# One full-height product and one paired product in the fold of an attention block

## What is computed

```
W = weights[condition]                          # (B, 32, 32)
h = einsum('bct,bcd->bdt', x, W)
q_c = h @ Wq_c.T + bq_c                         # 192 query latents
q = q_c @ Wq_up.T + bq_up                       # 32 heads of 128 + 64
kv = h @ Wkv_c.T + bkv_c                        # 64 latents + 64 rotary
k = [kv_nope @ Wk_up.T, kv_rope];  v = kv_nope @ Wv_up.T
out = softmax(q @ k.T / sqrt(192)) @ v @ Wo.T + bo
```

## Time and profile before

| | |
|---|---|
| Median of 3 runs | 732.34 us (731.35 to 732.41) |
| The profiled execution | 729.96 us, span 728.1 us |
| Mean granted TensorE clock over the span | 0.998 |
| Busy, share of the span | PE 97%, PEld 78%, DVE 83%, ACT 57%, POOL 29% |
| The chain that ended last | PE 72%, DVE 15%, of it line L729 32% |
| Matmuls of the fold (L729) | 2304 |

### The profile page before, as it was taken

One profiled execution on the slowest core, in us unless ns is written; L12 is line 12 of the kernel. 1 busy time (PEld: TensorE's weight loads), 2 busy tenths in 40 slices (PEclk: granted clock), 3 DMA queues, 4 the chain that ended last, 5 costly groups with the idle time before them and its releaser, 6 DMA issues.

```text
span 728.1 us, 17041 instructions
## 1 busy us (share of the span) xinstructions
PE 705.8 (97%) x7154; PEld 567.8 (78%) x7154; DVE 601.3 (83%) x1010; ACT 412.7 (57%) x736; POOL 208.1 (29%) x237
## 2 busy tenths in 40 slices
PE   8999999999999999999999999999988899999997
PEld 6867777786978697777878786978666688888885
DVE  4889999998999777797769776787889689999975
ACT  4676565656556765746475565656645444444443
POOL 5461020020002010640110000004300257777784
PEclk9999999999999999999999999999999999999999
DMA  7800100010002001000100010002112487989943
GB/s 225 322 3 2 58 7 1 2 62 3 1 2 62 3 2 49 11 5 13 59 5 1 2 59 2 2 1 92 59 60 54 121 234 147 187 236 196 238 104 109
DMA packets 31919, 50.94 MB, mean 70 GB/s; under 512 B 6594, under 2 KB 21090, under 8 KB 30562
## 3 DMA queue, kind: packets, MB, share of 16 engines
q1 hardware_dynamic: 29858, 49.26, 25.0%
q0 software_dynamic: 1024, 0.53, 0.3%
q10 hardware_dynamic: 960, 0.06, 0.1%
HBM read 41.19 MB, written 8.63 MB: 68 GB/s over the span
## 4 chain that ended last, share of the span: by engine, by line
PE 72%; DVE 15%; issue 4%; ACT 4%; DMA 3%; POOL 2%; SPq 0%; DVEq 0%; ACTq 0%; POOLq 0%
PE ps L729 32%; PE ps L778 6%; PE ps L621 5%; PE ps L622 5%; PE ps L623 5%; PE ps L800 4%; PE ps L670 3%; PE ps L629 2%; PE ps L631 2%; PE ps L630 2%; DVE x_low L1654 2%; DVE x_t L1648 2%; PE ps L1022 1%; PE ps L1030 1%; DMA x_t<-in_x_channels 1%
## 5 line engine op out<-in xcount | busy, mean ns | idle before, releaser
L1134 ACT ACTIVATE qt<-ps,m_bias 128x512 f32<-128x512 f32 x228 | 145.9, 687 | 87.7 <-PE ps L729 86.9
L729 PE MATMUL ps<-q_high,m_high 64*128 64x512 f32 x768 | 165.0, 397 | 0.0
L729 PE MATMUL ps<-q_high,m_low 64*128 64x512 f32 x768 | 161.3, 387 | 0.0
L729 PE MATMUL ps<-q_low,m_high 64*128 64x512 f32 x768 | 113.8, 387 | 0.0
L729 PEld LDWEIGHTS ps<-q_high,m_high 64*128 64x128 f32 x768 | 88.7, 184 | 15.0 <-issue 5.5
L729 PEld LDWEIGHTS ps<-q_high,m_low 64*128 64x128 f32 x768 | 88.8, 184 | 9.2
L1422 DVE TENSOR_TENSOR z_low<-ps,z_high 128x512 fp32r<-128x512 f32 x128 | 79.8, 683 | 18.1 <-ACT z_high L1154 16.5
L729 PEld LDWEIGHTS ps<-q_low,m_high 64*128 64x128 f32 x768 | 81.1, 184 | 10.2
L1154 ACT CAST z_high<-ps 128x512 fp32r<-128x512 f32 x128 | 66.8, 597 | 14.6 <-PE ps L800 9.8
L1139 ACT ACTIVATE sc<-sc 128x512 f32<-128x512 f32 x60 | 38.1, 635 | 41.5 <-DVE sc L1407 41.4
L494 POOL TENSOR_TENSOR o_sum<-o_part,o_part 128x512 f32<-128x512 f32 x7 | 9.1, 1300 | 173.2 <-ACT o_part L1164 173.2
(11 more groups left out here) (259 smaller groups left out, 1468.7 us busy)
## 6 DMA issues: line engine op xcount, KB each, us to landing
x_raw<-in_x_groups SPq DMA_DIRECT2D x32, 256.0 KB, 4.0
x_t<-in_x_channels SPq DMA_DIRECT2D x8, 1024.0 KB, 7.9
out<-rest SPq DMA_DIRECT2D x32, 256.0 KB, 6.3
toep_high<-taps_scratch SPq DMA_DIRECT2D x32, 192.0 KB, 4.5
toep_low<-taps_scratch SPq DMA_DIRECT2D x32, 192.0 KB, 4.9
w_raw<-in_w_groups SPq DMA_DIRECT2D x8, 512.0 KB, 7.5
toep_far<-taps_scratch SPq DMA_DIRECT2D x32, 64.0 KB, 5.7
rope_raw<-in_rope_rows SPq DMA_DIRECT2D x8, 192.0 KB, 7.4
```

What stands on the lines that cost most here:

```text
L729: mm = pe.matmul(ps[:, fold_bank(u, j) + e, :], weights[rows, (GH * g + j) // 2, c, :], moving[c][rows, :], start=start, stop=stop)
L1134: act.activation(qt[:, j, :], ps[:, fold_bank(u, j) + j % 2, :], ACT.Identity, bias=m_bias[:, h:h + 1]).then_inc(s["qt_done"], 1)
```

## The change

The 192 latents of a head become one piece of 128 and one of 64. The piece of 128 is a full-height matmul for each head (`full`, L737 of the changed kernel); the last 64 of two heads are a pair on the two halves (`paired`, L743). A couple is 6 full-height matmuls and 3 pairs. `q_high` and `q_low` are one tile each for the first 128 latents; `qc_high` and `qc_low` hold the last 64 on both halves. They are mixed once for each token: the even features go to rows 0 to 63 and the odd ones to rows 64 to 127 of PSUM (L675), and ACT and DVE then cross 64 rows of 256 elements instead of 512. The second copy of 64 feature columns goes. The weight products become four of full height and four of half (L706, L709), and the host's layouts follow. The waits of the first fold on `q_done` and `q_crossed` move behind the full-height matmuls.

```diff
-    feat = t("feat", [P, 4, 64 + FEAT], at=qt_at + 24 * KB)
-    q_high, q_low = ([t(f"q_{part}{n}", [P, ST], F32R, at=(q_at + (2 * k + n) * 2 * KB if n < 2 else h_at + 2 * k * KB))
-                      for n in (0, 2, 1)] for k, part in enumerate(("high", "low")))
+    feat = t("feat", [P, 4, FEAT], at=qt_at + 24 * KB)
+    q_high, q_low, qc_high, qc_low = (t(name, [P, ST], F32R, at=q_at + 2 * n * KB) for n, name in
+                                      enumerate(("q_high", "q_low", "qc_high", "qc_low")))
...
+    halves = lambda tile: tile[:].rearrange("p (m d c) -> p d m c", d=2, c=P)
+    weight_of = lambda tile, h, slot: tile[:, 2 * (h // 4) + slot // 3, slot % 3, :]
...
-                for part, made in enumerate(("q_ready", "qca_ready", "kv_ready")):
-                    for n in range(4):
-                        mm = pe.matmul(mixed_in(part)[:, P * n:P * n + P], feat[:, n, P * part:P * part + P],
-                                       mix[n // 2][:, n % 2, :], start=True, stop=True)
-                    mm.then_inc(s[made], 1)
+                for n in range(4):
+                    mm = pe.matmul(mixed_in(0)[:, P * n:P * n + P], feat[:, n, 0:P], mix[n // 2][:, n % 2, :],
+                                   start=True, stop=True)
+                mm.then_inc(s["q_ready"], 1)
+                for n in range(4):
+                    mm = pe.matmul(mixed_in(1)[64 * (n % 2):64 * (n % 2) + 64, P * (n // 2):P * (n // 2) + P],
+                                   feat[:, n, P:QL], mix[n // 2][:, n % 2, :], start=True, stop=True)
+                mm.then_inc(s["qc_ready"], 1)
+                for n in range(4):
+                    mm = pe.matmul(mixed_in(2)[:, P * n:P * n + P], feat[:, n, QL:FEAT], mix[n // 2][:, n % 2, :],
+                                   start=True, stop=True)
+                mm.then_inc(s["kv_ready"], 1)
...
-                for p in range(2):
-                    for c in range(3):
-                        for e in range(2):
-                            j, part = 2 * p + e, (c + e) % 3
-                            pe.matmul(ps[64 * e:64 * e + 64, bank, 64 * (3 * p + c):64 * (3 * p + c) + 64],
-                                      w_raw[g][:, QL * j + 64 * part:QL * j + 64 * part + 64],
-                                      w_raw[g][:, 4 * QL + KVL * j:4 * QL + KVL * (j + 1)], start=True, stop=True)
+                key = lambda j: w_raw[g][:, 4 * QL + KVL * j:4 * QL + KVL * (j + 1)]
+                for j in range(4):
+                    pe.matmul(ps[:, bank, 64 * j:64 * j + 64], w_raw[g][:, QL * j:QL * j + P], key(j), start=True, stop=True)
+                for j in range(4):
+                    e, p = j % 2, j // 2
+                    pe.matmul(ps[64 * e:64 * e + 64, bank, 256 + 64 * p:256 + 64 * p + 64],
+                              w_raw[g][:, QL * j + P:QL * j + QL], key(j), start=True, stop=True)
...
-                def both(j, weights, moving, c, start=False, stop=False):
+                def full(j, weights, moving, start=False):
+                    for e in range(2):
+                        pe.matmul(ps[:, fold_bank(u, j) + e, :], weight_of(weights, GH * g + j, j % 4 + e), moving[:],
+                                  start=start, stop=False)
+
+                def paired(j, weights, moving, stop=False):
                     for e in range(2):
                         rows = slice(64 * e, 64 * e + 64)
-                        mm = pe.matmul(ps[:, fold_bank(u, j) + e, :], weights[rows, (GH * g + j) // 2, c, :],
-                                       moving[c][rows, :], start=start, stop=stop)
+                        mm = pe.matmul(ps[:, fold_bank(u, j) + e, :], weight_of(weights, GH * g + j, 4 + j % 4 // 2)[rows, :],
+                                       moving[rows, :], start=False, stop=stop)
                         if stop:
                             mm.then_inc(s["t_ready"], 1)
 
@@ -738,24 +752,21 @@
                         pe.wait_ge(s["s_taken"], 4)
                     if u < 2 and j % 4 == 0:
                         pe.wait_ge(s["fold_done"], (GH * g + j) // 4 + 1)
-                    for c in (0, 2, 1):
-                        if c == 2 and g == 0 and j == 0:
-                            pe.wait_ge(s["q_high_done"], 2 * k + 2)
-                        if c == 1 and g == 0 and j == 0:
-                            pe.wait_ge(s["q_crossed"], 2 * k + 2)
-                        both(j, m_high, q_high, c, start=(c == 0))
-                        both(j, m_low, q_high, c)
+                    full(j, m_high, q_high, start=True)
+                    full(j, m_low, q_high)
 
                 def by_low(j):
-                    if g == 0 and j == 0:
+                    first = g == 0 and j == 0
+                    if first:
                         pe.wait_ge(s["q_done"], 2 * k + 1)
-                    both(j, m_high, q_low, 0)
-                    if g == 0 and j == 0:
-                        pe.wait_ge(s["q_done"], 2 * k + 2)
-                    both(j, m_high, q_low, 2)
-                    if g == 0 and j == 0:
+                    full(j, m_high, q_low)
+                    if first:
+                        pe.wait_ge(s["q_crossed"], 2 * k + 2)
+                    paired(j, m_high, qc_high)
+                    paired(j, m_low, qc_high)
+                    if first:
                         pe.wait_ge(s["q_copied"], 2 * k + 2)
-                    both(j, m_high, q_low, 1, stop=True)
+                    paired(j, m_high, qc_low, stop=True)
...
-                act.copy(feat[:, n, 64:64 + FEAT], ps[:, FEAT_BANK[n], 0:FEAT])
-                act.copy(feat[:, n, 0:64], ps[:, FEAT_BANK[n], P:QL]).then_inc(s["feat_done"], 1)
+                act.copy(feat[:, n, :], ps[:, FEAT_BANK[n], 0:FEAT]).then_inc(s["feat_done"], 1)
...
-            def projected_ca(k):
-                act.wait_ge(s["qca_ready"], k + 1)
-                act.activation(q_high[2][:], mixed_in(1), ACT.Identity,
-                               bias=bq_c[:, 1:2]).then_inc(s["q_high_done"], 1)
+            def projected_c(k):
+                act.wait_ge(s["qc_ready"], k + 1)
+                for e in range(2):
+                    rows = slice(64 * e, 64 * e + 64)
+                    made = act.activation(halves(qc_high)[rows, e],
+                                          mixed_in(1)[rows, 0:HALF].rearrange("p (m c) -> p m c", c=P), ACT.Identity,
+                                          bias=bq_c[rows, 1:2])
+                made.then_inc(s["q_high_done"], 1)
 
             def crossed(k):
                 act.wait_ge(s["q_high_done"], 2 * k + 2)
-                act.copy(q_high[1][64:P, :], f(q_high[2][0:64, :])).then_inc(s["q_crossed"], 1)
-                act.copy(q_high[1][0:64, :], f(q_high[0][64:P, :])).then_inc(s["q_crossed"], 1)
+                for e in range(2):
+                    here, there = slice(64 * e, 64 * e + 64), slice(64 - 64 * e, P - 64 * e)
+                    act.copy(halves(qc_high)[there, e], f(halves(qc_high)[here, e])).then_inc(s["q_crossed"], 1)
...
                 dve.wait_ge(s["q_high_done"], 2 * k + 2)
-                dve.scalar_tensor_tensor(out=q_low[2][:], in0=mixed_in(1), scalar=bq_c[:, 1:2],
-                                         in1=f(q_high[2][:]), op0=ALU.add,
-                                         op1=ALU.subtract).then_inc(s["q_done"], 1)
+                for e in range(2):
+                    rows = slice(64 * e, 64 * e + 64)
+                    made = dve.scalar_tensor_tensor(out=halves(qc_low)[rows, e],
+                                                    in0=mixed_in(1)[rows, 0:HALF].rearrange("p (m c) -> p m c", c=P),
+                                                    scalar=bq_c[rows, 1:2], in1=f(halves(qc_high)[rows, e]), op0=ALU.add,
+                                                    op1=ALU.subtract)
+                made.then_inc(s["q_done"], 1)
 
             def crossed(k):
                 dve.wait_ge(s["q_done"], 2 * k + 2)
-                dve.tensor_copy(q_low[1][64:P, :], f(q_low[2][0:64, :])).then_inc(s["q_copied"], 1)
-                dve.tensor_copy(q_low[1][0:64, :], f(q_low[0][64:P, :])).then_inc(s["q_copied"], 1)
+                for e in range(2):
+                    here, there = slice(64 * e, 64 * e + 64), slice(64 - 64 * e, P - 64 * e)
+                    dve.tensor_copy(halves(qc_low)[there, e], f(halves(qc_low)[here, e])).then_inc(s["q_copied"], 1)
...
-    laid["wcT"] = np.concatenate([q_c[64:], q_c[:64], kv_c]).reshape(FEAT, TT, P).transpose(2, 1, 0)
+    laid["wcT"] = np.concatenate([q_c, kv_c]).reshape(FEAT, TT, P).transpose(2, 1, 0)
...
-    rope = wq[:, NOPE:].reshape(NPAIR, 2, ROPE, 3, 64).transpose(1, 4, 0, 3, 2)
-    laid["rope_rows"] = np.stack([rope[0], np.roll(rope[1], -1, axis=2)]).reshape(P, NPAIR, 3, 64)
+    rope = wq[:, NOPE:].transpose(0, 2, 1).reshape(QUADS, 4, QL, ROPE)
```

(42 more changed lines are left out.)

## The result

The changed kernel takes **774.34 us** (median of 4 runs, 772.79 to 776.65) against 731.85 us of the kernel before beside it (730.92 to 732.41). The ratio is 1.059, with a 95% interval from 1.0571 to 1.0609: slower by 5.9%. The forecast was 773.8 us in 766 to 781.

A forecast was written before the change was run, and what follows sets the result against it. PE's matmul steps were taken to bound units 2 to 14. Changes of form +36.2, unit 0 +4.6, unit 1 +2.6, mixing -2.3 and unit 15 +0.4 sum to 41.5 us; on the 732.34 median, 773.8 us, range 766 to 781.

The forecast's parts named there:

- What bounds: Units 2 to 14: time is what PE needs, from matmul start to start; work taken from ScalarE or VectorE is worth nothing.
- Slots at 0: Fold: a full-height matmul and a half-height pair each take one 0.227 us slot; 9 slots before and after, cost 0.
- 0.20 us a change, 181 changes, +36.2 us: Folds of units 2 to 14: each switch between 128*128 and 64*128 matmuls costs 0.20 us extra, all on the path.
- Mixing -0.25 us each: Each of 7 later mixings: 16 full and 8 half-width passes plus two changes of form, 2.4 us against 2.6 to 2.7.
- First mixing -0.5 us: First mixing: saves 0.5 us, more than the others, since the granted clock is 0.65 there and a pass takes longer.
- Products +0.55 us a group: Weight products before the folds: 1.3 us a group where they took 0.75; five groups on the path, +2.8 us.
- Unit 1, +1.2 us beyond its products and with its mixing: Unit 1: VectorE sets the end, hiding part of PE's 3.9 us; +2.6 us in all, +1.2 when sorted by place.
- Unit 15, +0.4 us: Unit 15: VectorE's 2.85 us wait covers earlier changes of form; two couples behind it pay one change each, +0.4 us.
- the drainless one: Rival: changes between 128*128 and 64*128 cost nothing as weights load ahead; 729.8 us, faster; 3%.
- half the price: Rival: only the 0.09 us wait before a new form shows; 16.3 us in place of 36.2, 752 us; 4%.
- the dearer change of 0.25 us: Rival: both halves of a pair must finish before a full-height matmul; +12 us, 786 us; 3%.
- Loads shown at each full-height step: Rival: weight loads add 0.11 us at each of 640 more full-height steps; +70 us, 844 us; 1%.

The follow-up runs named there:

- two_full: Kernel before, with the first two of a couple's 9 half-height pairs replaced by two adjacent full-height matmuls; values not the reference's: 773.07 us, ratio 1.0584.
- all_full: Kernel before, with each of the fold's 9 half-height pairs replaced by one full-height matmul; values not the reference's: 726.83 us, ratio 0.995.
- serpentine: Changed kernel, with every second couple of heads folded in the opposite order, pairs first: 755.52 us, ratio 1.033.
- half_products: Changed kernel, with each weight product of 128 weight columns made as two of 64 side by side: 769.84 us, ratio 1.0546.

## Why the prediction was right

- *What bounds*: PE's chain in units 2 to 14. Right: ScalarE's idle time before `qt` rose by 47 us, and the period of two units went from 66.90 to 72.77 us, where 72.2 was forecast: the fold's loss came through whole. The smaller copies of ScalarE and VectorE were costed at 0 there. No run takes them by themselves; two_full, which keeps the old copies and has the same 181 changes, is 1.3 us dearer in these units than the changed kernel with its mixings taken out (39.4 against 38.1), so they can't have been worth much more than that.
- *Slots at 0*: right. all_full shows it by itself, 0.227 us a step.
- *0.20 us a change, 181 changes, +36.2 us*: right in kind and 5% low. With the mixings taken out the changes cost 38.1 us, 0.21 each. The two first steps are what the earlier trace rows had, though the way back was put together there from two other changes (64*128 to 32*64, and the transposes to 128*128); it measured 0.33 and 0.33 to 0.34. What the sum left out is that the slots behind a change are a little longer (below). The range had up to 0.21.
- *Mixing -0.25 us each*: -0.11 measured, 2.48 us after 2.59. Two sizes were off. A pass of 64 weight columns, two side by side in 0.109 us, is 0.055 and not 0.045. Of the two changes, the one before L675 costs 0.15 as taken (by the single starts in the trace, steps of 0.205 and 0.161), but the one before L679 0.20 (0.208 and 0.214 after steady steps of 0.109 and 0.112). This and the change's price are why units 2 to 14 lost 2.7 us more than forecast.
- *First mixing -0.5 us*: it took 2.67 us and not 4.3, a gain of 1.6, because the granted clock was 1.00 there and not 0.65 as in the earlier trace rows. The serpentine's profile has 0.56 in 15 to 18 us and half_products' 1.00. So this differs between executions and is no effect of the change; it flatters the changed kernel's unit 0 by over a microsecond.
- *Products +0.55 us a group*: 0.57 measured. half_products takes it back: 3.8 us less in unit 0 of its profile and 3.2 by the ratios, where five to seven groups are 2.9 to 4.0.
- *Unit 1, +1.2 us beyond its products and with its mixing*: +1.8 measured. The scores started directly behind the value products, as foreseen, and VectorE, not PE, was the one that waited: its late head there stands idle for 1.73 us.

```profile
74.27 1.21 PE L811 MATMUL ps<-pT,ctok 32*64 32x128 f32 x64
75.40 1.92 PE L789 MATMUL ps<-qt,kv 128*32 128x512 f32 x16
...
74.41 0.75 DVE L1448 TENSOR_SCALAR qt<-ps,m_bias 128x512 f32<-128x512 f32 x1 [1.73 <-PE ps L743]
```

- *Unit 15, +0.4 us*: +0.4. The wait of 2.85 us shrank to 1.50, so it took up what came before it:

```profile
586.80 1.20 PE L811 MATMUL ps<-pT,ctok 32*64 32x128 f32 x64 [1.50 <-DVE sc_last L1615]
```

- That the total came within 0.6 us is partly luck. Between the two profiled executions the loss is 43.8 us and not 41.5: units 2 to 14 came out 2.7 us dearer and unit 1 0.6, unit 0 1.1 us cheaper. The medians are 42.5 us apart, because the profiled execution of the kernel before, 729.96 us, was faster than all four of its runs beside the changed one; and the forecast was added to 732.34, where these four have a median of 731.85. The upper end of the range, 781, is also 1.4 us more than the terms named for it add up to.
- The rivals: the drainless one and half the price fall by the timelines and the table, and so does the dearer change of 0.25 us, as none of the four kernels with added changes has more than 0.218. Loads shown at each full-height step fall by all_full, whose 1152 full-height matmuls show none; here the Trainium skill's rule in "TensorE: Matmul & The Clock Gate", Part 3 (overlap only where the row group differs) disagrees with the measurement, and the measurement decides. That a change of tiling mode drains the engine (the Trainium skill, "TensorEngine Tiling (Array Packing)", Tiling Modes) agrees in kind with the loads that aren't taken ahead at a change, and here it has a price. The clock stayed at 1.00.

## What to carry to other kernels

Count changes of form, not only slots: two half-height matmuls side by side are worth one full-height one, but every move between the two forms cost 0.21 us here, nearly one whole slot of 512 columns. Look for it in the weight loads: one that starts together with its own matmul, and not one slot ahead, marks a change. A split into full-height and half-height parts pays only where long runs of each form stand together; if they must alternate, reverse every second group so that like follows like. And read such a price from starts at an existing change in the trace of before: here four rows gave the largest term to 5%.

## What was not expected

- Behind a change the steps stay longer for some slots: in the changed kernel from 173.43 to 173.90 two slots take 0.46 us, 0.232 each, where all_full has 0.227. That is some 0.03 us for a couple, and it is the 5% by which a change was dearer than its first two steps. Its cause was not tried.
- A full-height slot alone between pairs has 0.43 us to the next start, against 0.33 where a second full-height one stands before the change. That one step holds the second part of the change into it (0.11 us) and the first part of the change out of it (0.09), so the two changes still sum to 0.41 us.
- all_full is 0.5% faster than the kernel before. By its profile units 2 to 14 take 1.5 us less, which one change fewer doesn't explain, and unit 15 and the rest 1.3 us less (201.76 us), while unit 0 takes 1.7 us more with the stop and the half clock shown above. Its 12 runs lie apart in two groups, 724.1 to 725.3 and 728.4 to 730.9 us, and the profiled one, 729.09, is of the second. It computes something else, and the gain was not followed up.
